# The sixth product's sums on VectorE, and one quarter of the fifth product moved ahead of it

## The reference

```python
x = x + 0.5 * ffn(layernorm(x))          # x: 4 tiles of 512 tokens x 512 features, float32
x = x + attn(layernorm(x))               # z = x @ W.T; per feature four decaying sums over the tokens;
                                         # h = z + sum_k eta[k] * m_k; layernorm(h) * gamma + beta
x = x + 0.5 * ffn(layernorm(x))
# ffn(x): gated = silu(x @ w_gate.T) * (x @ w_up.T)      hidden size 2048
#         return gated @ w_down.T
```

## Time and profile before

| | us |
|---|---|
| median of three runs | 1025.83 |
| the profiled execution | 1025.42 |
| its span, first to last instruction | 1023.6 |
| TensorE busy | 1009.7 (99%) |
| VectorE busy | 726.9 (71%) |
| ScalarE busy | 426.2 (42%) |
| GpSimd busy | 201.1 (20%) |

### The profile page before, as it was taken

How to read it: one execution, slowest core, us unless ns; L and a number is a source line. 1 busy time by engine, 2 the same in 40 slices (tenths; PEclk the granted TensorE clock), 3 DMA queues, 4 the chain that set the end, 5 groups by cost and what they waited for, 6 DMA issues and landing times.

```text
span 1023.6 us, 13275 instructions
## 1 busy us (share of the span) xinstructions
PE 1009.7 (99%) x4796; PEld 851.3 (83%) x4796; DVE 726.9 (71%) x1063; ACT 426.2 (42%) x681; POOL 201.1 (20%) x223
## 2 busy tenths in 40 slices
PE   8999999999999999999999999999999999999798
PEld 7888888888888888888888888888888888888698
DVE  7756666598989687858888868785784566544943
ACT  6644545465423623225632362322382334333430
POOL 4123343124300200210440020021031133100400
PEclk9999999999999999999999999999999999999899
DMA  6688877678667555547856764464677799853255
GB/s 206 233 322 318 304 265 254 236 237 267 237 233 241 166 191 169 191 135 254 271 173 228 238 204 153 137 202 143 225 254 255 271 330 333 308 195 106 71 185 185
DMA packets 75792, 228.41 MB, mean 223 GB/s; under 512 B 6608, under 2 KB 25040, under 8 KB 68048
## 3 DMA queue, kind: packets, MB, share of 16 engines
q1 hardware_dynamic: 75152, 226.52, 65.1%
q10 hardware_dynamic: 576, 1.05, 0.3%
HBM read 173.02 MB, written 54.53 MB: 222 GB/s over the span
## 4 chain that ended last, share of the span: by engine, by line
PE 97%; DVE 2%; DMA 0%; issue 0%; ACT 0%; POOL 0%; DVEq 0%; ACTq 0%
PE ps_a L1799 8%; PE ps_a L1800 8%; PE ps_a L1798 8%; PE ps_b L1798 7%; PE ps_b L1799 7%; PE ps_b L1800 7%; PE ps_d L1798 7%; PE ps_d L1799 7%; PE ps_d L1800 7%; PE ps_c L1800 6%; PE ps_c L1799 6%; PE ps_c L1798 6%; PE aux L1800 3%; PE aux L1798 3%; PE aux L1799 3%; PE ps_d L2005 1%
## 5 line engine op out<-in xcount | busy, mean ns | idle before, releaser
L1224 DVE TENSOR_TENSOR tmp<-tmp,ps_c 128x512 f32<-128x512 f32 x59 | 40.4, 684 | 119.9 <-PE ps_c L1800 119.8
L1798 PE MATMUL ps_a<-xt,gu 128*128 128x512 f32 x304 | 118.5, 390 | 0.0
L1799 PE MATMUL ps_a<-xt,gu 128*128 128x512 f32 x304 | 118.5, 390 | 0.0
L1800 PE MATMUL ps_a<-xt,gu 128*128 128x512 f32 x304 | 118.4, 390 | 0.0
L1799 PE MATMUL ps_b<-xt,gu 128*128 128x512 f32 x286 | 111.5, 390 | 0.0
L1798 PE MATMUL ps_b<-xt,gu 128*128 128x512 f32 x286 | 111.5, 390 | 0.0
L1800 PE MATMUL ps_b<-xt,gu 128*128 128x512 f32 x286 | 111.4, 390 | 0.0
L1798 PE MATMUL ps_d<-dn,hid 128*128 128x512 f32 (+1 forms) x256 | 92.9, 363 | 0.0
L1800 PE MATMUL ps_d<-dn,hid 128*128 128x512 f32 (+1 forms) x256 | 92.9, 363 | 0.0
L1799 PE MATMUL ps_d<-dn,hid 128*128 128x512 f32 (+1 forms) x256 | 92.9, 363 | 0.0
L1800 PE MATMUL ps_c<-xt,gu 128*128 128x512 f32 x236 | 92.0, 390 | 0.0
(11 more groups left out here) (275 smaller groups left out, 2338.5 us busy)
## 6 DMA issues: line engine op xcount, KB each, us to landing
dn<-dn_kept SPq DMA_DIRECT2D x92, 512.0 KB, 4.1
gu<-gu_kept SPq DMA_DIRECT2D x46, 1024.0 KB, 5.1
gu<-gu_kept SPq DMA_DIRECT2D x46, 768.0 KB, 5.6
gu_kept<-gu SPq DMA_DIRECT2D x14, 1024.0 KB, 4.6
gu_kept<-gu SPq DMA_DIRECT2D x14, 768.0 KB, 4.2
dn_kept<-dn SPq DMA_DIRECT2D x16, 512.0 KB, 5.1
t_kept<-zx SPq DMA_DIRECT2D x16, 512.0 KB, 4.8
dn<-t_kept SPq DMA_DIRECT2D x16, 512.0 KB, 4.5
```

The source lines that it names most:

```text
L1224: dve.tensor_tensor(dst, u3s(si), p5_bank(si)[:, :], ALU.add).then_inc(c22_done, 1)
L1798: pe.matmul(dst, a_hi, b_hi, start=start, stop=False, skip_group_check=chained)
L1799: pe.matmul(dst, a_hi, b_lo, start=False, stop=False, skip_group_check=chained)
L1800: return pe.matmul(dst, a_lo, b_hi, start=False, stop=stop, skip_group_check=chained)
```

## The change

The sums S2 go from GpSimd's list to VectorE's. `s_of` is cut into `s3_of`, `s1_of` and `s4_of`, which are called one after the other in the sets, as before, and apart from each other for pair 7. `s2_of(i)` waits for S3 of its pairs alone, and ScalarE's high part of a quarter of Q6 waits for its S2 alone. Quarter 2 of Q5 moves ahead of the four quarters of Q6, and quarter 3 stays behind them. Behind the sets VectorE's list is written anew; the adds of Q6 and Q5 come after the low parts 8 and 10 in place of 7 and 9.

```diff
--- before.py
+++ after.py
@@ -62,7 +62,7 @@
     LAST = PH - 1
     SEG = 32 * LAST
     STAGES = (B11, B21, T2, T3, T1, T4, B22)
-    ENDING = ([(Q5, 0), (Q5, 1)] + [(Q6, i) for i in range(4)] + [(Q5, 2), (Q5, 3)]
+    ENDING = ([(Q5, 0), (Q5, 1), (Q5, 2)] + [(Q6, i) for i in range(4)] + [(Q5, 3)]
               + [(w, i) for w in (Q7, Q3, Q4) for i in range(4)])
     ENDED = (Q6, Q5, Q7, Q3, Q4)
     assert tokens == 512 and D == 512 and DT == ST == 4 and HT == 16 and tiles == 4 and K == 4
@@ -915,9 +915,10 @@
                     act.wait_ge(done, upto(SETS * PH - 1))
                 else:
                     act.wait_ge(batch_done, n - len(STAGES) + 1)
-                act.wait_ge(s_step, 4 * (2 * i + 1) + (2 if w == Q5 else 4))
                 if w == Q6:
                     act.wait_ge(s2_step, i + 1)
+                else:
+                    act.wait_ge(s_step, 4 * (2 * i + 1) + (2 if w == Q5 else 4))
                 act.copy(xt[:, stage_op(n), 0, :, :], stage_rows(w, i)).then_inc(stage_hi, 1)
 
             def load_silu():
@@ -1101,15 +1102,6 @@
                 pool.wait_ge(t_sums, 4 * j + 3)
                 pool.tensor_tensor(t[:, 3, :], b21, t[:, 2, :], ALU.subtract).then_inc(t_sums, 1)
 
-            def s2_of(i):
-
-                pool.wait_ge(s_step, 4 * (2 * i + 2))
-                if i == 0:
-                    pool.wait_ge(hid1_done, 16 * PH)
-                    pool.wait_ge(hid21_done, 8 * PH)
-                pool.tensor_tensor(s2_rows(i), hid1[:, 4 * i + 1:4 * i + 4:2, :], first_rows(i, 0), ALU.subtract
-                                   ).then_inc(s2_step, 1)
-
             def rstd_x(k, c):
                 pool.wait_ge(lnx_ve_done, 4 * k + c + 1)
                 r = units_of(k, c)
@@ -1204,8 +1196,6 @@
                 place_second(p + 1)
             for j in range(PAIRS):
                 t_sums_of(j)
-            for i in range(4):
-                s2_of(i)
 
         @block.vector
         def _(dve):
@@ -1324,18 +1314,33 @@
                 dve.wait_ge(t_hi, j + 1)
                 dve.tensor_tensor(t_part(1), t_raw(), t_part(0).bitcast(F32), ALU.subtract).then_inc(t_lo, 1)
 
-            def s_of(q):
-
-                tile1_even, tile1_odd = hid1[:, 2 * q, :], hid1[:, 2 * q + 1, :]
-                s3, s4 = first_row(q, 0), first_row(q, 1)
+            def s3_of(q):
+
                 dve.wait_ge(hid1_done, 16 * LAST + 2 * q + 2)
                 dve.wait_ge(lo0_ready, 16 * LAST + 2 * q + 2)
-                dve.tensor_tensor(s3, s3, tile1_even, ALU.subtract).then_inc(s_step, 1)
-                dve.tensor_tensor(tile1_even, tile1_even, tile1_odd, ALU.add).then_inc(s_step, 1)
+                dve.tensor_tensor(first_row(q, 0), first_row(q, 0), hid1[:, 2 * q, :], ALU.subtract).then_inc(s_step, 1)
+
+            def s1_of(q):
+
+                dve.tensor_tensor(hid1[:, 2 * q, :], hid1[:, 2 * q, :], hid1[:, 2 * q + 1, :], ALU.add
+                                  ).then_inc(s_step, 1)
+
+            def s4_of(q):
+
+                s4 = first_row(q, 1)
                 dve.wait_ge(s_step, 4 * q + 1)
-                dve.tensor_tensor(s4, s4, s3, ALU.add).then_inc(s_step, 1)
+                dve.tensor_tensor(s4, s4, first_row(q, 0), ALU.add).then_inc(s_step, 1)
                 dve.wait_ge(s_step, 4 * q + 3)
-                dve.tensor_tensor(s4, s4, tile1_odd, ALU.subtract).then_inc(s_step, 1)
+                dve.tensor_tensor(s4, s4, hid1[:, 2 * q + 1, :], ALU.subtract).then_inc(s_step, 1)
+
+            def s2_of(i):
+
+                if i == 0:
+                    dve.wait_ge(hid1_done, 16 * PH)
+                    dve.wait_ge(hid21_done, 8 * PH)
+                dve.wait_ge(s_step, 4 * (2 * i + 1) + 1)
+                dve.tensor_tensor(s2_rows(i), hid1[:, 4 * i + 1:4 * i + 4:2, :], first_rows(i, 0), ALU.subtract
+                                  ).then_inc(s2_step, 1)
 
             def stage_lo_of(n):
                 w, i = ENDING[n]
@@ -1568,7 +1573,9 @@
                 if p == 0:
                     gu_lo_a(si + 1)
                 if p == LAST and si % 2 == 0:
-                    s_of(si // 2 - 1)
+                    s3_of(si // 2 - 1)
+                    s1_of(si // 2 - 1)
+                    s4_of(si // 2 - 1)
                 if p in (1, 2):
                     if si in (2, 3, 6):
                         scan_begin(p, {2: 0, 3: 1, 6: 3}[si])
@@ -1777,18 +1784,27 @@
                     window(p)
 
             stage_lo_of(1)
-            s_of(PAIRS - 1)
             stage_lo_of(2)
+            s2_of(0)
+            s3_of(PAIRS - 1)
             for b in range(2):
                 add_block(x_ps, b, 2, 0, first_done, 2 * PAIRS - 1)
             stage_lo_of(3)
+            s2_of(1)
+            s2_of(2)
+            stage_lo_of(4)
+            s2_of(3)
+            stage_lo_of(5)
+            s1_of(PAIRS - 1)
+            stage_lo_of(6)
+            s4_of(PAIRS - 1)
             for b in range(2):
                 add_block(y_ps, b, 2, 0, first_done, 2 * PAIRS, b + 1)
-            stage_lo_of(4)
-            for n in range(5, 20):
+            for n in range(7, 20):
                 stage_lo_of(n)
-                if n in (7, 9, 13, 17):
-                    add_product({7: Q6, 9: Q5, 13: Q7, 17: Q3}[n])
+                if n in (8, 10, 13, 17):
+
+                    add_product({8: Q6, 10: Q5, 13: Q7, 17: Q3}[n])
             add_product(Q4)
 
         @block.tensor
```

## The result

The changed kernel takes 1016.07 us (median of 4 runs, 1015.84 to 1016.41) beside 1025.67 us for the kernel before; the ratio is 0.9907, 95% interval 0.9890 to 0.9924. The forecast was 1016.1 us in a range of 1015.0 to 1018.4, faster with a chance of 0.96. The profiled execution took 1016.25 us.

What follows compares the result with a forecast made beforehand. The prediction took TensorE to bound the kernel, paused near the end by GpSimd's sums and VectorE operations they stretch. Pause 7.79 plus half clock 1.82 gave 9.61 us saved: 1016.1 us, range 1015.0 to 1018.4.

Steps and rivals of the forecast that it cites:

- The pause: TensorE's wait ahead of (Q6, 0), from 958.69 to 966.48, goes whole: 7.79 us.
- The clock: The 18 matmuls behind the pause, at half clock before, run at full clock: 1.82 us gained.
- The chain (c): VectorE's new list of operations behind the sets, each start time given, from 954.85 to 970.16.
- the margin at (Q6, 1): Least slack of a low part before TensorE wants it: 0.8 us, 0.66 behind the semaphore.
- The cover (e): Adds of Q6 have one batch of Q5 beside them instead of two, before (Q7, 0); cost nothing.
- The fetches (f): Weight fetches near the end have three batches, 8.64 us, and land 3.5 to 5.8 us after issue; cost nothing.
- Rival 3: VectorE is slow in the end stretch for another reason than GpSimd: 1037 us, slower than before; chance 0.03.
- rivals 1, 2 and 4: At the end: some pause stays, 1017.3 us (0.10); clock falls anyway, 1018 (0.03); TensorE loses pace, about 1021 (0.02).

Runs made afterwards that it cites:

- the three kernels with GpSimd beside: The changed kernel with four sums, sixteen memsets or eight copies added on GpSimd that nobody waits for: 1024.50, 1016.22 and 1022.48 us.
- the three sums more: The changed kernel with three more 128x1024 sums on VectorE ahead of the low part of (Q6, 1): 1019.20 us.
- the order alone: The changed kernel, with its new batch order and weaker waits, but S2 made on GpSimd: 1020.43 us.
- GpSimd's sums beside: The changed kernel with four 128x1024 sums on GpSimd behind the sets, into rows that nobody reads: 1024.50 us.

## Why the prediction was right

- The pause: 7.79 us predicted, and none is left. That VectorE's operations would be back at 0.69 and S2 cost 1.22, the low end of 1.21 to 3.4, decided it. It was argued from the ends of the long operations, 0.55 us behind GpSimd's; the three kernels with GpSimd beside show it.
- The clock: 1.82 predicted from 18 matmuls; measured alone, 1.76 in the profiles and 1.9 to 2.2 in the medians.
- The chain (c) came true within 0.05 us at every step, once the shift of 0.47 is taken off; the margin at (Q6, 1) was 0.77 for 0.80 before the semaphore, and 0.57 to 0.64 behind it by the three sums more, for 0.66.
- The cover (e): enough, and worth 1.1 us where it is missing, as the 1.0 worked out from the add.
- The fetches (f): 3.3 to 4.2 us, where 8.64 were allowed. The prediction names rows 12 for them and rows 11 for the cover (e); it is the other way round, and the numbers are read rightly.
- Rival 3, the slower side, falls with the operations of pair 7 at 0.69 in the same place; rivals 1, 2 and 4 with a TensorE that never waits and a clock of 1.00.
- The last tenth is luck: 9.60 us measured beside a sum of 9.61 is closer than the runs of either kernel agree among themselves (some 0.5 us), and 1016.1 was chosen between 1015.8 and 1016.2.

Two of the expectations had the total nearly right and its parts less so. With the order alone I had 2.9 us of pause at (Q6, 0) and 0.5 at (Q6, 1), with the clock as a possibility; it was the 2.9 and the fall, and the slower TensorE then asked for (Q6, 1) when it was ready. With GpSimd's sums beside, the 0.5 us at (Q6, 1) went the same way.

The Trainium skill, page SBUF — State Buffer, section "SBUF: two separate sides", says that GpSimd blocks a VectorE operation with two SBUF inputs only when it reads SBUF itself, and whoever is first holds the ports for its whole instruction. The runs agree: beside GpSimd's sums VectorE's operations take 2.83 to 3.42 us and beside its copies 1.52 to 2.06, for what takes 0.69 to 1.22 alone and beside the memsets; the added time, 2.1 to 2.2 and 0.83 us, goes with the length of the GpSimd operation, and the adds, with an input in PSUM and so outside the rule, are unchanged.

## What to carry to other kernels

Work on GpSimd that reads SBUF is not free while VectorE has work with two SBUF inputs that somebody waits for: in these runs each such VectorE operation ended one GpSimd operation later, whether or not anyone needed GpSimd's result. Moving the sums over to VectorE made the sums shorter (four at 1.22 us for four at 2.8 to 3.3) and VectorE's own operations too (0.69 for 2.8 to 2.9). When an order is written out by hand, put down for each batch when its operand is ready and when it is wanted; the least difference is where the next microsecond is lost, and a batch of another bank behind a product covers the adds that free its own.

## What the runs showed of the hardware

- GpSimd memsets of 128x1024 (0.95 us) leave VectorE's two-input operations alone; copies of 128x1024 (1.05 at the fastest) lengthen them by 0.83 us, sums by 2.1 to 2.2 (0.9 where the last sum was half over).
- Of two pauses of TensorE of nearly the same length, 2.77 and 2.73 us, the granted clock fell behind one (0.71 over the next 5.13 us, 32 matmuls) and not behind the other (1.00, 43 matmuls); in each of the two kernels one run of four has the mean clock of the other case. Behind 2.87 us, with a pause of 1.78 shortly before, it was 0.62 over 4.46 us; behind 6.0 and 7.6 us 0.51 and 0.50, the lower level.
- The arrival of the first input differs by 0.3 us between executions, which shifts everything behind it.
